# Attention layer with feed-forward: weighting bursts change places between even and odd units, and VectorE's small steps move behind later maxima

## Time and profile before

| | |
|---|---|
| runs | 1063.99 us (1063.72 to 1064.26) |
| the profiled execution | 1064.13 us, span 1062.3 us |
| TensorE (PE) busy | 1026.5 us, 97% of the span |
| VectorE (DVE) busy | 809.5 us, 76% |
| ScalarE (ACT) busy | 665.1 us, 63% |
| GpSimd (POOL) busy | 266.2 us, 25% |
| chain that ended last | PE 80%, DVE 10%, ACT 6% |
| granted TensorE clock | 0.99 to 1.00 of full speed |

### The profile page before, as it was taken

The page is one execution under the profiler, slowest core; times in us unless marked ns, Lnnn a source line. Parts: engine busy times, 40 slices in busy tenths (PEclk is TensorE's granted clock), DMA queues, the critical chain, the costliest instruction groups (busy, mean ns, idle before and its releaser), DMA issues.

```text
span 1062.3 us, 15699 instructions
## 1 busy us (share of the span) xinstructions
PE 1026.5 (97%) x5858; PEld 536.8 (51%) x5858; DVE 809.5 (76%) x1199; ACT 665.1 (63%) x1346; POOL 266.2 (25%) x227
## 2 busy tenths in 40 slices
PE   8999999999999999999999999999999999999996
PEld 3643344433443433443444443333337888888885
DVE  4899978899779799779988899999803475662535
ACT  2368877788778788778766678888863431222221
POOL 2751030141335422246200042844100000000002
PEclk9999999999999999999999999999999999999999
DMA  5274417243142512344140446531217510402011
GB/s 200 80 196 126 106 35 213 52 97 78 52 115 75 105 56 54 82 108 105 34 78 12 116 120 150 124 121 37 93 68 193 166 40 9 111 28 52 1 39 42
DMA packets 64432, 94.87 MB, mean 89 GB/s; under 512 B 37536, under 2 KB 37920, under 8 KB 62272
## 3 DMA queue, kind: packets, MB, share of 16 engines
q1 hardware_dynamic: 63776, 93.10, 33.2%
q10 hardware_dynamic: 576, 0.72, 0.2%
HBM read 53.95 MB, written 27.00 MB: 76 GB/s over the span
## 4 chain that ended last, share of the span: by engine, by line
PE 80%; DVE 10%; ACT 6%; issue 2%; DMA 1%; SPq 0%; POOL 0%; DVEq 0%; POOLq 0%
PE PS L448 21%; PE PV L467 20%; PE PSA L537 15%; PE PS L554 5%; PE PSA L426 5%; DVE nmx L964 5%; PE PS L365 4%; ACT Bn L756 3%; PE PS L493 2%; PE PSA L493 2%; DVE nmx L960 2%; DVE nmx L957 2%; ACT Bn L765 2%; PE PV L554 2%; PE PSA L365 1%
## 5 line engine op out<-in xcount | busy, mean ns | idle before, releaser
L756 ACT ACTIVATE Bn<-PS 128x512 f32<-128x512 f32 x1146 | 548.8, 559 | 125.0 <-PE PS L448 111.1
L448 PE MATMUL PS<-Qt,Kt 50*128 50x512 f32 x1146 | 391.7, 434 | 20.0 <-ACT Bn L756 18.7
L426 PE MATMUL PSA<-Kt,Qt 48*128 48x512 f32 x1024 | 390.0, 459 | 2.2 <-DVE Kt L936 0.8
L964 DVE TENSOR_REDUCE nmx<-PSA 128x1 f32<-128x1024 f32 x256 | 312.2, 1219 | 61.0 <-PE PSA L426 59.8
L448 PEld LDWEIGHTS PS<-Qt,Kt 50*128 50x128 f32 x1146 | 184.4, 184 | 323.6 <-ACT Bn L756 312.7
L467 PE MATMUL PV<-Bn 128*32 128x512 f32 x2048 | 272.8, 605 | 0.0
L426 PEld LDWEIGHTS PSA<-Kt,Qt 48*128 48x128 f32 x1024 | 174.6, 183 | 21.7 <-DVE nmx L964 6.2
L960 DVE TENSOR_REDUCE nmx<-PSA 128x1 f32<-128x512 f32 x256 | 174.5, 682 | 1.4 <-PE PSA L426 1.1
L957 DVE TENSOR_REDUCE nmx<-PSA 128x1 f32<-128x512 f32 x256 | 174.3, 681 | 0.0
L537 PE MATMUL PSA<-x1Th,wr 128*128 128x512 f32 x344 | 135.0, 393 | 0.8 <-DVE sg L1052 0.5
L537 PE MATMUL PSA<-x1Tl,wr 128*128 128x512 f32 x344 | 134.7, 392 | 0.0
(11 more groups left out here) (166 smaller groups left out, 919.4 us busy)
## 6 DMA issues: line engine op xcount, KB each, us to landing
Qt<-pscr SPq DMA_DIRECT2D x90, 128.0 KB, 4.9
A<-in_wf SPq DMA_DIRECT2D x11, 768.0 KB, 6.3
wr<-A SPq DMA_DIRECT2D x33, 256.0 KB, 2.9
pscr<-A SPq DMA_DIRECT2D x16, 512.0 KB, 3.7
vscr<-Bn SPq DMA_DIRECT2D x32, 256.0 KB, 2.0
Kt<-pscr SPq DMA_DIRECT2D x90, 64.0 KB, 2.3
A<-A SPq DMA_DIRECT2D x16, 256.0 KB, 3.7
Bn<-vscr SPq DMA_DIRECT2D x8, 512.0 KB
```

Source lines behind the costliest of these rows:

```text
L426: op = e.matmul(PSA[:, 2 * s + h, :], Qt[n % 3][p:p + NC_, g % 2, 128 * qt:128 * qt + 128], Kt[n % 3][p:p + NC_, 512 * h:512 * h + 512], s ...
L448: e.matmul(PS2[:, i, cols], Kt[n % 3][rows, 128 * kt:128 * kt + 128], Qt[n % 3][rows, g % 2, 512 * qh + cols.start:512 * qh + cols.stop], ...
L756: e.activation(Pb[c % NP_][:, cols], PS2[:, score_bank[c, p], cols], ACT.Exp, scale=0.25).then_inc(*act_exp.next(piece(c, p)))
L964: e.tensor_reduce(nmx[:, hh % 2, c0:c0 + 1], slot_pair(s), AX.XY, ALU.max, negate=True).then_inc(*dve_max[s].next(k))
```

## The change

It is one change in five places.

1. The burst stands behind g = 3 in even units and behind g = 2 in odd ones, and the score tile in two pieces moves from even to odd units. Background work follows the burst directly, so in its (odd) units it now stands ahead of g = 3. ScalarE's `evacuate_raw` moves with it, behind the exponential of g = 2. VectorE's `first_norm`, `add_values` and `add_rows` stand between the two halves of the unit's second tile.
2. The casts `h0` and `h1` stand in even units, two units apart; for the projections of `project_at` they come one and two units later than before (h0 +7, h1 +9, out +10).
3. `reciprocal` stands at u % 8 = 5 (`recip_at`), `divide` four units behind it.
4. `gather` stands at u % 8 = 5.
5. `turn_max` is taken apart into `join_max`, `high_max`, `lower_max` and `turn_max`. The join stays behind the last maximum of a half head; the other three stand behind the first three maxima of the next half head, one each. `write_max` is issued at u % 8 = 4, one unit later.

```diff
-                    (0, 4): (1, "rope"), (0, 7): (1, "h0"), (0, 9): (1, "h1"), (0, 10): (1, "out")}
+                    (0, 4): (1, "rope"), (0, 8): (1, "h0"), (0, 10): (1, "h1"), (0, 11): (1, "out")}
         for at_u, j in project_at.items():
-            u0 = 16 * at_u[0] + at_u[1] + 6
-            rope_end.update({divmod(u0, 16): (j, "h0"), divmod(u0 + 1, 16): (j, "h1"), divmod(u0 + 2, 16): (j, "out")})
+            u0 = 16 * at_u[0] + at_u[1] + 7
+            rope_end.update({divmod(u0, 16): (j, "h0"), divmod(u0 + 2, 16): (j, "h1"), divmod(u0 + 3, 16): (j, "out")})
...
-        recip_at = {(2, 11): 0, (4, 11): 1, (6, 3): 2, (8, 3): 3, (10, 3): 4, (12, 6): 5, (14, 6): 6}
-        gather_at = {(n, {0: 13, 6: 5}.get(n, 3)): n + 2 for n in range(NG - 2)}
+        recip_at = {(2, 13): 0, (4, 13): 1, (6, 5): 2, (8, 5): 3, (10, 5): 4, (12, 5): 5, (14, 5): 6}
+        divide_at = {divmod(16 * n + v + 4, 16): kc for (n, v), kc in recip_at.items()}
+        gather_at = {(n, {0: 13}.get(n, 5)): n + 2 for n in range(NG - 2)}
...
+        def apart(hh):
+
+            return 1 <= hh < 2 * NG - 1
...
-            return [slice(0, 128), slice(128, 512)] if c % 8 == 3 and c < 4 * SPLIT else [slice(0, 512)]
+            return [slice(0, 128), slice(128, 512)] if c % 8 == 7 and c < 4 * SPLIT else [slice(0, 512)]
...
-            last = score_bank[4 * u + 3, len(pieces(4 * u + 3)) - 1]
+            last = score_bank[4 * u + 2, 0]
...
-                    if u >= 1 and g == (2, 3)[u % 2]:
+                    if u >= 1 and g == (3, 2)[u % 2]:
                         weigh(u - 1)
...
+                        background(u)
...
                     exponent(u, g)
+                    if g == 2 and at_u in project_at:
+                        for h, i in enumerate(free_banks(u)):
+                            evacuate_raw(project_at[at_u], h, i)
                 if u >= 1:
                     finish(u - 1)
-                if at_u in project_at:
-                    for h, i in enumerate(free_banks(u)):
-                        evacuate_raw(project_at[at_u], h, i)
...
-                if k % 16 == 15:
-                    turn_max(hh)
-
-            def turn_max(hh):
+                if 1 in halves and k % 16 == 15:
+                    join_max(hh)
+                    if not apart(hh):
+                        high_max(hh)
+                        lower_max(hh)
+                        turn_max(hh)
+                if 1 in halves and k > 16 and k % 16 < 3 and apart(hh - 1):
+                    (high_max, lower_max, turn_max)[k % 16](hh - 1)
...
-                maximum(next(steps))
-                if at_u in norm_at:
-                    first_norm(False, 0, norm_at[at_u])
...
+                k = next(steps)
+                if at_u in norm_at or at_u in out_at or at_u == values_at:
+                    maximum(k, (0,))
+                    if at_u in norm_at:
+                        first_norm(False, 0, norm_at[at_u])
...
+                    maximum(k, (1,))
+                else:
+                    maximum(k)
...
-                if steps_done(u) // 16 > steps_done(u - 1) // 16:
+                if u % 8 == 4:
                     write_max(steps_done(u) // 16 - 1)
+                if u == SPLIT - 1:
+                    write_max(2 * NG - 1)
```

More of the change, by code:

```diff
@@ L665, in tensor, with background @@
                     project_half(1, 1, 3, ((0, 1), (2, 3))[k - 2])
+            def background(u):
+                at_u, pair = divmod(u, 16), free_banks(u)
+                if at_u in project_at:
+                    for h, i in enumerate(pair):
+                        project_half(project_at[at_u], h, i, (0, 1, 2, 3))
+                if at_u == values_at:
+                    for t in range(8):
+                        value_rows(1, t, pair[t // 4])
+                if at_u in out_at:
+                    t2 = out_at[at_u]
+                    out_project(False, 0, t2, [bank(i) for i in pair], [bank_free[i] for i in pair])
+                    for j, i in enumerate(pair):
+                        bank_free[i] = dve_y.at((False, 0, 2 * t2 + j))
             for u in range(SPLIT):
@@ L945, in add_values, with maximum @@
                     ALU.add).then_inc(*dve_val.next((b, h)))
-            def maximum(k):
+            def maximum(k, halves=(0, 1)):
                 if k >= len(stream):
@@ L955, in maximum @@
                 if by_halves(k):
[L956 to L961, removed]
+                    for h in halves:
+                        w.wait_ge(*pe_max.at((k, 0) if h == 0 else k))
+                        col = nmx[:, hh % 2, c0 + 16 * (h == 0):c0 + 16 * (h == 0) + 1]
+                        e.tensor_reduce(col, slot_pair(s)[:, h, :], AX.X, ALU.max, negate=True).then_inc(
+                            *dve_max[s].next((k, 0) if h == 0 else k))
                 else:
@@ L973, in turn_max, with high_max @@
                 e.tensor_tensor(top[:, 0:8], top[:, 0:8], rest, ALU.min).then_inc(*dve_ms.next(("join", hh)))
+            def high_max(hh):
                 w.wait_ge(*dve_ms.at(("join", hh)))
@@ L976, in turn_max, with lower_max @@
                     w.wait_ge(*dve_ms.at(("turn", hh - 1)))
-                e.tensor_copy(msp[:, 0:16], top).then_inc(*dve_ms.next(("high", hh)))
+                e.tensor_copy(msp[:, 0:16], nmx[:, hh % 2, 0:16]).then_inc(*dve_ms.next(("high", hh)))
+            def lower_max(hh):
                 w.wait_ge(*dve_ms.at(("high", hh)))
-                e.tensor_tensor(msp[:, 16:32], top, msp[:, 0:16].bitcast(F32), ALU.subtract).then_inc(
+                e.tensor_tensor(msp[:, 16:32], nmx[:, hh % 2, 0:16], msp[:, 0:16].bitcast(F32), ALU.subtract).then_inc(
                     *dve_ms.next(("low", hh)))
+            def turn_max(hh):
                 w.wait_ge(*dve_ms.at(("low", hh)))
@@ L1218, in vector @@
                 maximum(next(steps))
-                maximum(next(steps))
-                if at_u in norm_at:
-                    first_norm(False, 0, norm_at[at_u])
[L1222 to L1226, removed]
+                k = next(steps)
[3 more added lines that the diff above has]
+                        first_norm(False, 0, norm_at[at_u])
+                    if at_u == values_at:
+                        for h, i in enumerate(free_banks(u)):
+                            add_values(1, h, i)
+                    if at_u in out_at:
+                        add_rows(False, 0, out_at[at_u], [bank(i) for i in free_banks(u)])
+                    maximum(k, (1,))
+                else:
+                    maximum(k)
                 if at_u in recip_at:
@@ L1414, in gpsimd @@
                     rope(project_at[at_u])
-                if at_u in recip_at:
-                    divide(recip_at[at_u])
+                if at_u in divide_at:
+                    divide(divide_at[at_u])
                 if at_u in rope_end:
```

3 lines of the change are left out of this document (1 added, 2 removed).

## The result

The changed kernel takes 1052.9 us (median of 5 runs, 1050.49 to 1056.92), against 1063.72 us (1063.64 to 1064.26) for the kernel before on the same chip: a ratio of 0.990, interval 0.9873 to 0.9927. That is 10.8 us faster, where 20 were forecast, and its runs lie 6.4 us apart, where those of before lie 0.6 apart. The profiled execution took 1055.03 us, span 1053.2.

A forecast was written before the change was run, and what follows sets the result against it. TensorE's order was taken to set the time (80% of the chain), with VectorE and ScalarE cutting in. From 1064.1: -14.7 - 3.0 - 5.7 + 1.9 + 1.4 = -20.1, so 1044.0 us; range 1040 to 1053.

The forecast's parts named there:

- The copy: The copy of `PV` falls into ScalarE's idle 0.54 behind the exchanged burst: 0.49 each, 30 times, 14.7 us off.
- The rival that it only changes its place: TensorE's burst end reaches ScalarE 0.3 late, or the next accumulation waits: 9 us come back, 1053; chance 0.08.
- Casts: Both casts of a projection fall into ScalarE's idle 0.54: six projections at 0.5 each, 3.0 us off.
- The four small steps: VectorE's small instructions behind a half head no longer stand as one block: 14 x 0.41, 5.7 us off.
- the residual of 0.1 a half head: Lag left by the spread small VectorE steps: 0.1 in 19 half heads without background, 1.9 us on, range 0 to 7.6.
- Reciprocals and background: Seven VectorE reciprocals cost 0.2 each, 1.4 us on (0 to 3.8); background work nets 0, -3 to +3.
- Later rows: Maxima's rows through DRAM after the later transposition need 4.3 of 4.8 us before the first score: nothing lost.
- The maxima's rows come too late: At `max_in` before each half head's first score, usual trips of 6.5 us make it slower: 1095; late rows' chance 0.05.
- `divide` later on GpSimd is not waited for by anything: nothing: Moving `divide` later on GpSimd costs nothing, since nothing in the loop waits for it.
- steps that cost 0.2 each: Rival that VectorE becomes the bound: small steps at 0.2 add 5.7, reciprocals show whole (+2.4), 1052; chance 0.14.
- a wait of TensorE on `max_in`: Sign of being wrong: in the changed kernel TensorE should never wait at the first score of unit 8h.

## Why the prediction was right or wrong

**The copy: right.** 29 of the 30 copies in the loop lie beside TensorE's work; the first stands on the chain together with a cast (the 3.50 of half head 1). The groups around the others are 1.88 to 1.91 and 3.04 to 3.06 instead of 3.53, but for those that the late rows and their low clock made longer. A plain half head lost 0.9 of its 20.66: the 0.49 of the copy and the 0.41 of the block. The rival that it only changes its place falls.

**Casts: right in what they no longer cost, wrong in what they start.** No cast of the six projections is on the chain. The first pair, units 1 and 2, kept its 3.56; the first cast of job 1 met the copy in unit 8 of head 0 and cost 0.45, which the term didn't have.

**The four small steps: right, and better than taken.** The 0.41 came off in undisturbed half heads, where the pace is 4.94 a pair to the end; the residual of 0.1 a half head didn't come. Worked from the fences above, the four take 0.35 instead of 0.76, and VectorE's busy time per plain half head fell from some 19.6 to 19.3 us. The Trainium skill's "The DRAIN you can't avoid" ("VectorE: DVE Perf Modes"), as the prediction read it, would have had them cost as much apart as together, 1049.7; here the trace decides against that reading. The section itself adds that a next instruction that isn't held starts earlier, and the 0.07 to 0.12 here beside 0.20 in a block agrees with that.

**Reciprocals and background: right.** 0.25 visible in half heads 24 and 28, 0.1 in the five with background, against 0.2 taken for each of seven. Half heads with background went from 26.3 or 26.4 to 25.9 or 26.0, those with a cast from 26.8 or 26.9 to 25.8 or 26.0: the copy's gain, the cast's, and next to nothing else.

**Later rows: the step that failed first.** The prediction wrote "4.3, half a microsecond inside: nothing". As a usual trip that is right: 29 of 30 took about 2 us, and the transposition ends 4.9 us ahead of the first score (673.85 and 678.75), where 4.8 was forecast. But it priced the usual trip and not the worst. Its own had the worst, 6.30 at the same half head (the trip before it took 4.27, 635.86 to 640.13), and it set that aside ("A single late one costs a few us") instead of asking what had hidden it. SyncE's timeline of the kernel before, 630 to 670 us:

```profile
640.74 2.62 SPq L1496 DMA_DIRECT2D Kt<-pscr  x6
...
654.49 0.43 SPq L1458 DMA_DIRECT2D A<-in_wf  x1
```

And the first score behind it, in the chain of waits, 650 to 680 us:

```profile
665.26 0.42 PE PS L448
```

From the first transfer of `gather` to the reads behind the next write are 22.1 us here (640.74 to 662.81), 21.8 in the changed kernel (633.34 to 655.10) and 22.4 with the steps in one block (633.50 to 655.94). Before, the last load was issued only 2.0 us ahead of the write (654.49), but the first score came 24.5 us behind `gather`, late enough for these rows. In the changed kernel `gather` stands two units later, and the score was due 20.1 behind it, at 653.5 (633.72, the first score one half head earlier, and 19.76). That room is what the change spends. The prediction priced `gather` by who needs its data ("serves maxima that begin fifteen units later"), and its "SyncE issues the loads of unit 5 behind this trip" looked at the loads that follow; the transfers that delayed the write had been issued ahead of it. Without two of the loads there the trip took 1.98 again. The transfers in between are not all the same in the three traces, and no run puts `gather` alone back, so this account of the room is worked out from times and not tested, and how the loss divides between the move of `gather` and the loads is not shown. Cost in the profiled run: 5.5 us, 4.1 in the group that waits (7.18 instead of 3.05) and 1.4 in the next, at 1.2 GHz (3.25 instead of 1.89). The rival "The maxima's rows come too late" had the mechanism and counted all 30 half heads; it was one.

**"`divide` later on GpSimd is not waited for by anything: nothing": the step that failed second**, and with it the casts' price. Both costed GpSimd's work by who waits for it. Nobody waits for it by a semaphore, and still it stops VectorE: casts in even units put the low part of a projection at the start of unit 5, where L997 now stands. In half head 13 `divide` itself had a part: it waited 4.99 for its data and ran until 365.36, and the first low part, whose cast on ScalarE had ended at 362.53, ran behind it, beside L987. Cost in the profiled run: 0.85 + 0.85 + 3.8 + 0.45 + 0.8 = 6.8 us, of which at most 1.7 is the low clock behind half head 13 (3.41 us at half speed). In the kernel before, none of these steps took more than 0.21, so no row showed it.

**The sum.** The profiled execution is 11.0 over the forecast of 1044.0. Late rows 5.5, holds 6.8 and job 1's cast 0.45 are 12.7; the split steps' residual that didn't come gives 1.9 back. That makes 10.8. Two other differences cancel and are no loss: the loop's first burst came 1.0 earlier (65.80 instead of 66.83), and the first half head of the last stage took 1.0 longer (24.65 instead of 23.67). Both are counted from the burst of an odd unit, which now stands one step earlier; from the first score of unit 240, which has kept its place, to the burst of unit 245 are 16.25 us, before 16.12. The kernel with both collisions moved away, 22.5 under before, is the forecast without its failed steps; it is 2.4 better than the 20.1 of the sum by the residual (1.9) and the cast of the first pair (0.5; half head 0 took 19.74 instead of 20.25).

**The range.** Its high end, 1053, came from two other rivals: steps that cost 0.2 each, and a copy that only changes its place. Neither came about, so that the median of 1052.9 lies just inside is luck, and the runs (1050.49 to 1056.92) lie on both sides. The late rows had their own rival only as an all-or-nothing case at 1095; a single late trip, which the prediction had seen and put at a few us, was in no bound, and holds were in none either. One of its own signs of being wrong did show: a wait of TensorE on `max_in`, 3.5 us, once.

## What to carry to other kernels

When a step moves later, look for the one slow instance of it in the trace of before and ask what hid it there; a median trip hides nothing. A transfer that moves later also moves closer to whatever is issued behind it, so price it by its place in the queue and not only by who needs its data. When a step moves onto an engine's critical place, list what the engine that shares its memory port runs at that time, even if no semaphore joins them, and give small steps a place where that engine is idle. A gain that varies from run to run more than the kernel before did is a sign of a collision, and moving the colliding work gave the other half of the gain here.

## What the runs showed of the hardware

**A small VectorE step waits for GpSimd to the end of its instruction.** Steps of 0.16 to 0.18 us that read and write SBUF took up to 1.27 beside a GpSimd instruction of 1.3 with two inputs; the cast, with one input, as well (1.16, 1.21). Reductions from PSUM (1.18 to 1.22) and the transposition (0.21) kept their time beside the same kind of work. The Trainium skill, "SBUF — State Buffer", section "SBUF: two separate sides", has a rule for this: VectorE and GpSimd share a pair of ports; between a GpSimd instruction and a VectorE one that has two SBUF inputs, or runs in a performance mode with two ports, whoever begins first has the pair for its whole instruction. The trace agrees for the steps with two inputs: GpSimd's three instructions began first in half head 13, and VectorE's steps ended within 0.03 us of them. In which mode the cast ran no run here shows.

**A small write can queue behind big ones on the way to DRAM**: 16 KB took 2.0 us, or 6.5 and with the steps in one block 9.3, by what was issued up to 15 us before it.

**A wait can cost twice.** After some of TensorE's waits of a few microseconds the granted clock was 0.50 for 3.4 or 6.8 us, in some runs and not in others; that costs at most 1.7 or 3.4 us, half of the stretch. Of the two profiled executions of the changed kernel, 1055.03 and 1050.75, one had such a stretch behind half head 13 and the other none, and that half head alone makes 3.0 of the 4.3 us between them (shorter holds are in it too).
